# Attention of a graph layer: quadratic forms in one bank, row sums, projections and splits at other steps

## The reference, cut to what matters

```python
xn = layernorm(x)                                  # 1250 nodes x 768, float32
h = xn @ W_gnn; out[col] += h[row] * dinv[row] * dinv[col]     # 20000 edges + loops
q, k, v = split(xn @ w_qkv + b_qkv)                # 12 heads of 64, q scaled by 1/8
A = q k^T; num = 1 + A + 0.5 * A * A
attn = num / num.sum(-1); mix = (attn @ v) @ w_proj + b_proj
x1 = x + gnn + mix
out = x1 + switch_ffn(layernorm(x1))               # 8 experts, top 1, capacity
```

## Time and profile before

| | |
|---|---|
| median of 3 runs | 1124.47 us (1123.52 to 1125.71) |
| profiled execution | 1128.61 us, its span 1126.9 us |
| TensorE busy | 935.3 us (83%) |
| VectorE busy | 732.6 us (65%) |
| ScalarE busy | 459.9 us (41%) |
| POOL busy | 314.1 us (28%) |
| six pairs | 141.7 to 631.3 us |
| mean granted TensorE clock | 0.923 |

### The profile page before, as it was taken

How to read it: one execution, slowest core, us unless ns; L and a number is a source line. 1 busy time by engine, 2 the same in 40 slices (tenths; PEclk the granted TensorE clock), 3 DMA queues, 4 the chain that set the end, 5 groups by cost and what they waited for, 6 DMA issues and landing times.

```text
span 1126.9 us, 15230 instructions
## 1 busy us (share of the span) xinstructions
PE 935.3 (83%) x5250; PEld 890.2 (79%) x5250; DVE 732.6 (65%) x1396; ACT 459.9 (41%) x678; POOL 314.1 (28%) x201
## 2 busy tenths in 40 slices
PE   3897789989989989989997689699999963399970
PEld 3896678888878888888886689699999963399960
DVE  6777169879879879879888445564545435166633
ACT  2311256666666666666677202110101030266520
POOL 2035545644645635633445000000000004000004
PEclk8898899999999999999999889799999965599995
DMA  9966443273273273398562664635353232879978
GB/s 279 315 170 151 76 78 60 24 152 60 23 151 60 26 149 60 48 204 200 121 139 51 92 153 95 164 96 136 95 136 94 80 110 61 235 233 279 282 192 273
DMA packets 143091, 152.24 MB, mean 135 GB/s; under 512 B 72205, under 2 KB 119926, under 8 KB 142024
## 3 DMA queue, kind: packets, MB, share of 16 engines
q1 hardware_dynamic: 114213, 137.46, 47.0%
q0 software_dynamic: 28432, 14.05, 9.5%
q10 hardware_dynamic: 403, 0.17, 0.1%
HBM read 105.79 MB, written 46.78 MB: 135 GB/s over the span
## 4 chain that ended last, share of the span: by engine, by line
PE 57%; DVE 16%; ACT 8%; issue 8%; DMA 6%; POOL 2%; SPq 1%; DVEq 0%; ACTq 0%; POOLq 0%
PE ps L1771 14%; PE ps L1773 13%; PE ps L1772 13%; PE ps L1157 6%; ACT Ph L803 3%; PE ps L1141 3%; PE ps L1142 3%; DVE Pl L1015 3%; ACT Pf L825 2%; DVE Ph L1013 2%; DMA rows<-oE 1%; POOL rows L1512 1%; PE ps L1405 1%; DMA Cs<-counts 1%; DVE eqp L968 1%
## 5 line engine op out<-in xcount | busy, mean ns | idle before, releaser
L363 POOL DMA_INDIRECT counts<-countc,idxu x157 | 278.9, 1777 | 315.1 <-DMA counts<-countc,idxu 244.7
L1015 DVE SCALAR_TENSOR_TENSOR Pl<-Pf,Ph 125x832 fp32r<-125x832 f32 (+1 forms) x180 | 184.4, 1026 | 65.1 <-ACT Ph L803 56.8
L825 ACT ACTIVATE Pf<-ps 125x832 f32<-125x832 f32 (+1 forms) x180 | 155.9, 867 | 145.9 <-PE ps L1142 139.8
L1157 PE MATMUL ps<-Ph,vsb 125*128 125x416 f32 (+1 forms) x360 | 131.9, 366 | 10.6 <-DVE Pl L1015 10.4
L1157 PE MATMUL ps<-Pl,vsb 125*128 125x416 f32 (+1 forms) x360 | 127.8, 355 | 0.0
L1512 POOL DMA_INDIRECT rows<-XF,slots x10 | 14.8, 1483 | 322.9 <-DVE slots L1627 320.2
L1771 PE MATMUL ps<-XH,wqkH 128*128 128x416 f32 (+1 forms) x216 | 81.7, 378 | 19.9 <-DVE R L933 10.2
L1771 PE MATMUL ps<-wH,XH 128*125 128x384 f32 x240 | 85.8, 357 | 9.9 <-DVE OHL L960 5.8
L1157 PEld LDWEIGHTS ps<-Ph,vsb 125*128 125x128 f32 x360 | 68.8, 191 | 20.6 <-DVE Pl L1015 10.1
L1772 PE MATMUL ps<-wL,XH 128*125 128x384 f32 x240 | 84.1, 351 | 0.0
L1773 PE MATMUL ps<-wH,XL 128*125 128x384 f32 x240 | 84.0, 350 | 0.0
(11 more groups left out here) (235 smaller groups left out, 2138.5 us busy)
## 6 DMA issues: line engine op xcount, KB each, us to landing
Cs<-counts SPq DMA_DIRECT2D x20, 546.9 KB
w1s<-L_ffn_w SPq DMA_DIRECT2D x8, 1152.0 KB, 8.8
w2s<-L_ffn_w SPq DMA_DIRECT2D x8, 1152.0 KB, 6.5
rows<-blank SPq DMA_DIRECT2D x2, 4215.0 KB
odram<-OHL SPq DMA_DIRECT2D x12, 625.0 KB, 8.6
oS<-odram SPq DMA_DIRECT2D x10, 750.0 KB, 4.9
vdram<-VS SPq DMA_DIRECT2D x10, 672.0 KB
vsb<-vdram SPq DMA_DIRECT2D x12, 560.0 KB
```

The lines of the kernel that those rows point to most:

```text
L363: pool.indirect_dma_start(out=counts, out_offset=bass.IndirectOffsetOnAxis(ap=idxu[:, c:c + 1], axis=0), in_=countc[:, c:c + 1], in_offset ...
L825: act.activation(Pf[:, i % RING, :, 0:w], ps[0:T, 2 * (i % 2):2 * (i % 2) + 2, 0:w], ACT.Square, bias=1.0).then_inc(sq_done, 1)
L1015: dve.scalar_tensor_tensor(out=p, in0=f, scalar=1.0, in1=h.bitcast(F32), op0=ALU.add, op1=ALU.subtract).then_inc(p_lo, 1)
L1157: ins = pe.matmul(ps[:, 4 + s % 2, 0:w], vsb[:, 2 * kp + t, a, :], part[:, m % RING, t, 0:w], start=(kp == 0 and t == 0 and part is Ph), s ...
```

## The change

The quadratic forms are made at steps 1, 5 and 9 instead of 3, 5 and 8, all in bank 6 (the second one was in bank 7); forms 1 and 2 each wait until the R before has been read out of the bank. The first projection of the next pair waits for the read of bank 7 at step 3 (`kq_full`) instead of R. The sums stand at 13, 14, 15 instead of 11, 12, 13, the turn of the inverse at 18 instead of 16. K's third chunk is projected a step earlier, the two chunks of Q a step later, and their reads and splits move with them; the second chunk of Q is split for the first head at step 0 of its own pair instead of 2.

```diff
--- before.py
+++ after.py
@@ -595,14 +595,14 @@
         END = STEPS + LAG + 3
 
 
-        QUAD_AT, TOTAL_AT, INVERSE_AT = (3, 5, 8), (11, 12, 13), 16
-        PROJ_AT, TURN_AT, GRAM_AT = (7, 13, 20, 24, 29), (24, 27, 30), 32
+        QUAD_AT, TOTAL_AT, INVERSE_AT = (1, 5, 9), (13, 14, 15), 18
+        PROJ_AT, TURN_AT, GRAM_AT = (7, 13, 19, 25, 30), (24, 27, 30), 32
         SLICES = 3
-        READ_AT = (11, 16, 23, 27, 32)
+        READ_AT = (11, 16, 22, 28, 33)
         OWN_READ_AT = 3
         SECOND_AT = (1, 3, 6, 9, 13, 18)
-        FIRST_AT = (24, 25, 26, 28)
-        LATE_AT = (2, 5)
+        FIRST_AT = (23, 25, 26, 29)
+        LATE_AT = (0, 5)
         WSPLIT_AT = (11, 25)
         FINISH_AT = (30, 32, END - 1)
 
@@ -930,7 +930,7 @@
 
                     c0, w = CHUNKS[c]
                     dve.wait_ge(gq_mm, 3 * j + (c + 1))
-                    dve.scalar_tensor_tensor(out=R32[:, c0:c0 + w], in0=ps[:, 6 + c % 2, 0:w], scalar=k1[:, 3:4],
+                    dve.scalar_tensor_tensor(out=R32[:, c0:c0 + w], in0=ps[:, 6, 0:w], scalar=k1[:, 3:4],
                                              in1=Q32[:, c0:c0 + w], op0=ALU.add, op1=ALU.mult).then_inc(r_done, 1)
 
                 def inverse():
@@ -1102,11 +1102,10 @@
                     if c == 0:
                         pe.wait_ge(kq_full, 6 * j + 4)
                         pe.wait_ge(gfin_done, j + 1)
-                    if c == 1:
-                        pe.wait_ge(kq_full, 6 * j + 6)
-                    if c == 2:
-                        pe.wait_ge(r_done, 3 * j + 1)
-                    pe.matmul(ps[:, 6 + c % 2, 0:w], gs[:, 2, :], Q32[:, c0:c0 + w], start=True,
+                    else:
+                        pe.wait_ge(kq_full, 6 * j + (4 + c))
+                        pe.wait_ge(r_done, 3 * j + c)
+                    pe.matmul(ps[:, 6, 0:w], gs[:, 2, :], Q32[:, c0:c0 + w], start=True,
                               stop=True).then_inc(gq_mm, 1)
 
                 def total(n):
@@ -1170,7 +1169,7 @@
                         g = max(g for g in range(5) if PROJ_AT[g] <= i)
                         part = i - PROJ_AT[g]
                         if i == PROJ_AT[0]:
-                            pe.wait_ge(r_done, 3 * j + 2)
+                            pe.wait_ge(kq_full, 6 * j + 6)
                         if part < SLICES:
                             project(j + 1, g, part * KT // SLICES, (part + 1) * KT // SLICES)
                     if not last and i in TURN_AT:
```

## The result

The kernel with the change takes 1115.44 us, median of five runs (1112.75 to 1117.69); the kernel before takes 1124.47 on the same chip (five, 1123.06 to 1125.71). The ratio is 0.9916, 95% interval 0.9894 to 0.9938: faster by 0.8%. 1114.5 was forecast, within 1109.5 to 1120. The profiled execution after took 1115.44 us for a span of 1113.7. The one before lay 4 us above its own median, so the two traces are 13.2 us apart where the medians are 9.0 apart: differences read from the traces are larger than what the change is worth.

A forecast was written before the change was run, and what follows sets the result against it. VectorE was taken to carry the first two thirds of a pair. Five loop pairs at 2.8 us (14.0), the last pair about 1 and clock about 0 made 15 us, about 10 arriving past the scatters: 1114.5, range 1109.5 to 1120.

The forecast's parts named there:

- (1): Q's second chunk split at step 0: TensorE's 1.50 us wait for MA before the scores of step 5 goes.
- (2): First quadratic form at step 1: a new 1.1 us wait for the Pl of step 2, bounds 0 and 1.5.
- (3): Forms in bank 6, projection freed of R: the 1.99 us wait goes; gain 2.6 to 2.8 us by step 10.
- (4): Sums at 13 to 15, form 2 at 9: new wait of about 1.0 us for step 10's Pl; gain 1.9 at step 16.
- (8): Granted clock: two falls in the pairs go, 2.6 us once; 2.5 set against that for new falls in the tail.
- (5): Inverse at step 18: TensorE waits 1.1 us for it where 0.4 stood; gain at step 19 is 2.1.
- (6): Later projections: K's third chunk fills a 0.5 us wait, gain 2.8 at step 23; Q's move into the tail 0.0 +- 0.3.
- (7): SP's queue, with the inverse's store two steps later: costs nothing, at most 2 us once.
- What of it arrives: Seam after the pairs: scatters keep Cs from loading before 624.7, so about 10 of the 15 us arrive.
- rival A: Scatters at the seam are no bound, faster pairs draw them along: all 15 to 18 us arrive, 1108; 8%.
- Rival B: VectorE keeps the gain or the tail's clock falls: 1 us or less per pair left, 1122; 14%.
- Rival C: Slower: a denser VectorE slows the issue of the scatters; 1141 with 0.3 us more each; 5%.

The follow-up runs named there:

- e5: Kernel before with Q's second chunk split at step 0, forms at steps 1, 5, 8 in bank 6, projection freed of R; 1107.98 us, ratio 0.9851.
- e1: Kernel before with only Q's second chunk split for the first head at step 0 instead of 2; 1127.45 us, ratio 1.0029.
- e2: Kernel before with only the forms at steps 1, 5, 8 in bank 6 and the projection freed of R; 1121.95 us, ratio 0.9977.
- e3: Kernel after with projections, reads and first-head splits of K's third and Q's two chunks back at their old steps; 1114.09 us, ratio 0.9911.
- e4: Kernel after with K's second chunk projected from step 12 instead of 13; 1109.42 us, ratio 0.9868.
- e6: e4 without the last 20 of the 157 scatters of edge counts; 1108.19 us, ratio 0.9868.
- e11: e5 with K's last turn at step 31, loop-pair finishes at 32 and 33, K's third chunk projected from step 19, inverse at 17; 1109.2 us, ratio 0.9854.
- e9: e5 with the sums at steps 13 to 15 instead of 11 to 13 and the inverse at 18 instead of 16; 1120.02 us, ratio 0.9957.

## Why the prediction was right, step by step

The number came out within 1 us by luck: two terms were wrong and their errors cancelled. By the traces the pairs gave 10 us where 15 were forecast, and all of it arrived, where only 10 of the 15 were to.

The step that failed in the pairs is the running sum that ends at 2.8 us a pair. Its own list of waits would have shown it. It has 1.1 for the Pl of step 2, 1.0 for the Pl of step 10, 1.1 for inv, 0.5 in step 30, 2.0 before the turn and 0.2 before the Gram product, 5.9 in all, where 7.4 stood. TensorE's work was taken as equal, so by this list a pair becomes about 1.5 shorter and not 2.8. The trace has waits of 5.8 and an undisturbed pair 1.6 shorter. The list is a rough measure, since busy time changes a little too: in pair 1 of e5 the waits are 2.1 less and the pair is 2.7 shorter. Step by step:

(1) Right: the wait for MA goes.

(2) Right: 1.11 for the Pl of step 2, where 1.1 was worked out; in the other loop pairs it is 0.87 to 1.05. e5 shows 1.20 in pair 1.

(3) Right for the change: the wait for R goes, and steps 0 to 9 are 2.6 to 2.8 shorter than in undisturbed pairs before, as forecast. e1 and e2 show what the prediction didn't say: neither edit is worth its own term. Each wait grows by 0.6 to 0.8 when the other goes, and only both together bring the gain. Both waits came from the same lateness of VectorE.

(4) The new wait was found, 1.23 where 1.0 was laid out, so about 1.5 was left at step 16 instead of 1.9. What it does to the clock was missed, see (8).

(5) Right for the wait: 1.02 for inv (forecast 1.1). The gain at step 19 is 1.7 instead of 2.1. The waits that (5) names (0.4 and 0.5 gone, 1.1 new) would lose 0.2, where it adds 0.2; the trace of pair 1 gains 0.2 there.

(6) Wrong in its main claim, that the later steps come out at 0.0 +- 0.3. 2.3 was left at step 23 in pair 1. From there to step 28, where the slices have moved, the five pairs lose 0.3 to 0.9 (0.7 in pair 1). TensorE waits 0.17 for a Pl there, at 280.11, and has a gap of 0.12 before the turn of K in step 27; the rest isn't seen as idle time. e3, with the projections at their old steps, loses nothing there. In the tail the waits are 0.59 and 1.66 (0.5 and 2.0 forecast) with none before the Gram product, and the stretch from step 29 to the pair's end takes 11.70, before 11.81.

(7) Nothing is seen of SP's queue, as forecast.

(8) About right in the sum, wrong in the place. I had two falls of the clock go, and set 2.5 against that for new ones in the tail. The two of the kernel before did go and none came in the tail; two came behind the new wait of (4). Behind the tail's longest wait, 1.66 in pair 1, the window from 296 to 299.5 has a clock of 1.00. TensorE's timeline in pair 3 of the kernel after, and windows there and in that tail:

```profile
411.93 0.42 PE L1156 MATMUL ps<-Ph,vsb 125*128 125x416 f32 x1 [1.30 <-DVE Pl L1015]
...
412.75 0.93 PE L1116 MATMUL ps<-blocks,R 128*125 128x2 f32 x8
413.55 0.44 PE L1770 MATMUL ps<-XH,wqkH 128*128 128x416 f32 x1
...
414.22 0.55 PE L1770 MATMUL ps<-XH,wqkH 128*128 128x416 f32 x1
```

```profile
410.50:414.00 3.50, 2.20 (x15) 2.10 (x15) 3.34 (x8) 2.90 (x5) 1.72 (x2) 1.00 0.24 0
414.10:417.60 3.50, 3.50 (x12) 3.32 (x11) 2.44 (x5) 0.72 (x1) 1.57 (x1) 0.51 0.14 3
417.60:421.00 3.40, 3.40 (x22) 3.36 (x22) 2.11 (x4) 1.23 (x3) 1.73 (x2) 1.00 0.52 113
...
296.00:299.50 3.50, 3.50 (x20) 3.47 (x21) 3.24 (x6) 0.80 (x2) 2.90 (x2) 1.00 0.12 0
```

TensorE waits 1.30 us at step 13, does four products and eight matmuls of two columns, and from 414.2 on the matmuls take 0.55 us. The window from 414.1 to 417.6 has a clock of 0.51, the level of 1.2 GHz, and before and behind it stands 1.00. The steps 13 and 14 of that pair take 5.56 + 4.60 where an undisturbed pair takes 5.06 + 3.55. That is 1.5 for each of two pairs. Without the wait (e5, where the sums stand earlier, and e4, where a slice stands ahead of the product) the clock stays at 1.00.

The pairs in sum: 14.0 were forecast for the five of the loop. The undisturbed ones gained 1.6 (82.6 to 81.0), and two falls before stand against two after: 8.3. The last pair gained 1.9 (forecast 1), and in it a wait for inv shrank from 1.7 to 0.3, which the prediction doesn't name. The remaining 2.7 of the 12.9 us between the last stores of the two traces lie before the first pair, in code that didn't change. The first pair starts anywhere from 138.9 to 141.7 over the profiles, so this is a difference between executions. The last stores at 618.4 lie behind the 613 to 617 expected, and the pairs of 80.6 to 82.5 above the 79.5 to 80.5, one of them only just.

What of it arrives: here the prediction was wrong. "Cs can't be loaded before 624.7" took one execution's end of the scatters for a floor. Over the twelve profiles with all scatters the last one ended anywhere from 594 to 622, with pairs fast or slow. In e5 it started at 601.3 while the pairs ended 20 us earlier than before. e6 bears it out: without the last twenty scatters the time is the same. And when the scatters did hold Cs (5.2 us in e4, 7.7 in e11), it came back in the load: I had 11 to 13.84 from Cs to the csum, and measured were 6.4 and 5.1. From the last stores to the csum it is 17 to 19 us in every profile, and from the csum to the end 474 to 478, so what the pairs gain arrives. TensorE idles 6.45 before the first degrees, not 13. Cs followed the parameter loads at once, which is the sign of rival A, held at 8%. The scatters are no bound, as it has it, but faster pairs don't draw them along either, and the pairs gave 10 in the traces and not its 15 to 18.

Rival B (VectorE keeps the gain) is in the shortfall: three waits for VectorE, 3.4 us of a pair, stand in the first two thirds. Rival C is out, since neither the time nor the scatters became slower. The scatters after:

```profile
L363 POOL DMA_INDIRECT counts<-countc,idxu x157: 1551/1587/2337, 69.2 to 611.1; - x157
```

The median was 1662 ns before and is 1587 here, the longest 2484 and 2337, while VectorE went 27 us without a gap of 0.2. Over the other kernels here the median is 1559 to 1668, so this difference says nothing of its own.

## What to carry to other kernels

Two waits of one engine for the same late engine, a few microseconds apart, can be one problem. Take away one and the other grows, so price and try the edits together before judging either. When work is moved off a busy stretch, look at what filled TensorE's time there: the sums in the steps 11 and 12 had hidden VectorE's lateness. Their move alone cost 12 us (e9), of which the one traced execution shows 6, and in the whole change a slice of projection in their place gave 5 back (e4). Check a running sum of gains against the list of waits it comes from: where the engine's work was equal, the two came within 0.6 us a pair here. A time at which a self-paced chain of transfers ended in one execution is no floor until a second execution has it too, and a load that was issued late may come back sooner.

## What the hardware showed unexpectedly

The granted clock fell behind waits of 1.24 and 1.30 us that were followed by four products and eight two-column matmuls (the kernel after, pairs 4 and 3), and behind 1.3 and 1.6 at the same place in e3 and e9. It fell in two loop pairs of five behind waits of 2.0 (the kernel before), and in most behind single waits of 2.3 to 2.7 (e1, e2). In the kernel after the wait of 1.66 before the turn of K left it at 1.00, and so did the waits of e5, 0.9 to 1.3, of which each pair has three. Which pairs are hit follows no difference in their waits: 1.30 and 1.24 in the two hit, 1.29, 1.23 and 1.29 in the three that were not. What decides it stays open; no run separates the length of the wait from the work behind it.

The load of the counts, small pieces from DRAM, took 5.1 and 6.4 us to the csum where it was issued late (e11, e4) and 12.3 to 13.8 right behind stores and parameters (the others). The Trainium skill (DMA: Bandwidth & Descriptors, "Issuing engines are not separate DMA queues") has transfers of all engines share the same 16 DMA engines and interleave. The two figures agree with that; no run separates the part of each transfer ahead.
